# Transposed counts of a graph kernel: stored by the count stage, or fetched with transposing transfers

## The reference, cut to what matters

```python
def _hconv(x, W, b, src, dst, n):
    xt = x @ W
    ...
    m = jax.ops.segment_sum(xt[src], dst, num_segments=n) * Binv[:, None]
    out = jax.ops.segment_sum(m[dst], src, num_segments=n) * Dinv[:, None]
    return out + b
...
h = _prelu(_hconv(x, W1, b1, src, dst, n), a)
h = _hconv(h, W2, b2, src, dst, n) + x
```

## Time and profile before

| | us |
|---|---|
| median of 3 runs | 1770.72 |
| lowest, highest | 1768.19, 1774.01 |
| span of the profiled execution | 1767.3 |
| TensorE busy | 1590.3 |
| ScalarE busy | 1095.2 |
| VectorE busy | 1068.9 |
| DMA queue of SP, share of 16 engines | 32.7% |

### The profile page before, as it was taken

How to read it: one execution, slowest core, us unless ns; L and a number is a source line. 1 busy time by engine, 2 the same in 40 slices (tenths; PEclk the granted TensorE clock), 3 DMA queues, 4 the chain that set the end, 5 groups by cost and what they waited for, 6 DMA issues and landing times. The chain is left out here.

```text
span 1767.3 us, 35592 instructions
## 1 busy us (share of the span) xinstructions
PE 1590.3 (90%) x11957; PEld 1399.6 (79%) x11957; DVE 1068.9 (60%) x1881; ACT 1095.2 (62%) x2024; POOL 81.8 (5%) x116
## 2 busy tenths in 40 slices
PE   5777677599999999998999799999999999999697
PEld 4666666599999999996666599997779999777465
DVE  5598898679999999997455411122322112677662
ACT  1377778688888888885333466656665555567221
POOL 3000000000000000002000100000000000111213
PEclk9888898799999999998999999999999999999899
DMA  7315555345121221303000144445554444557212
GB/s 203 95 62 169 160 160 154 96 129 141 25 68 46 58 62 38 75 1 76 13 1 0 41 111 122 123 108 140 129 136 125 124 122 108 146 155 175 70 28 55
DMA packets 137572, 170.06 MB, mean 96 GB/s; under 512 B 20374, under 2 KB 129099, under 8 KB 137448
## 3 DMA queue, kind: packets, MB, share of 16 engines
q1 hardware_dynamic: 127538, 155.61, 32.7%
q0 software_dynamic: 6368, 9.36, 2.1%
q10 hardware_dynamic: 3542, 3.46, 0.8%
HBM read 114.58 MB, written 53.76 MB: 95 GB/s over the span
## 5 line engine op out<-in xcount | busy, mean ns | idle before, releaser
L1611 PE MATMUL ps_sets<-arena,kinds_mem 125*125 125x195 bf16 (+1 forms) x2500 | 447.2, 247 | 24.6 <-DVE kinds_mem L1370 16.7
L1354 ACT ACTIVATE kinds_mem<-ed_rows,es_mask 125x625 bf16<-125x625 f32 x500 | 367.0, 810 | 59.2 <-PE ps_sets L1617 31.0
L1617 PE MATMUL ps_sets<-arena,kinds_mem 125*125 125x195 bf16 (+1 forms) x2300 | 396.9, 248 | 0.0
L1611 PEld LDWEIGHTS ps_sets<-arena,kinds_mem 125*125 125x125 bf16 x2500 | 342.5, 137 | 31.6 <-DVE kinds_mem L1370 23.6
L2800 ACT ACTIVATE onewide<-ring 125x625 fp32r (+1 forms) x325 | 222.5, 720 | 168.7 <-PE oneps L2517 95.0
L1617 PEld LDWEIGHTS ps_sets<-arena,kinds_mem 125*125 125x125 bf16 x2300 | 308.2, 134 | 0.0
L2489 PE MATMUL oneps<-onewide,parts_a 125*128 125x376 f32 (+1 forms) x2000 | 293.1, 308 | 8.3 <-DVEq L2580 8.3
L2489 PEld LDWEIGHTS oneps<-onewide,parts_a 125*128 125x128 f32 x2000 | 291.2, 190 | 9.2 <-DVEq L2578 8.7
L2517 PE MATMUL oneps<-oneparts_b,onewide 125*125 125x512 f32 x1000 | 234.6, 395 | 0.0
L2517 PEld LDWEIGHTS oneps<-oneparts_b,onewide 125*125 125x125 f32 x1000 | 184.5, 185 | 48.6 <-DVE onefull L2652 1.9
L1362 DVE TENSOR_TENSOR kinds_mem<-kinds_mem,blk 125x2500 bf16<-125x2500 bf16 x120 | 182.4, 1520 | 33.9 <-ACT kinds_mem L1354 28.8
(11 more groups left out here) (451 smaller groups left out, 1903.8 us busy)
## 6 DMA issues: line engine op xcount, KB each, us to landing
ring<-counts SPq DMA_DIRECT2D x50, 683.6 KB
ring<-countsT SPq DMA_DIRECT2D x40, 683.6 KB
countsT<-kinds_mem SPq DMA_DIRECT2D x25, 683.6 KB
blk<-counts SPq DMA_DIRECT2D x20, 546.9 KB
counts<-blk SPq DMA_DIRECT2D x3, 3418.0 KB
counts<-kinds_mem SPq DMA_DIRECT2D x2, 3418.0 KB
ed_rows<-ed_dram SPq DMA_DIRECT2D x16, 273.4 KB
ring<-countsT SPq DMA_DIRECT2D x10, 410.2 KB
```

What stands on the lines that cost most here:

```text
L1354: return k.nc.scalar.activation(kinds_of(k)[:, slot, 0, :], k.ed_b[:, h, :], ACT.Relu, scale=MASK_SCALE, bias=k.es_mask[:, t, h:h + 1])
L1611: t_.matmul(out[0], kind[0], z[0], start=(t == 0), stop=False)
L1617: last = t_.matmul(out[1], kind[1], z[1], start=False, stop=(t == T - 1))
```

## The change

The count stage no longer makes or stores transposed counts: L839, L774, L877 and their semaphores are gone, with ScalarE's wait for `tr_stored`. SP's block store now waits for ScalarE's last copy of the block (`blk_done`) directly. `counts` becomes 16 rows longer (`PAD_ROWS`); GpSimd clears a buffer of zeros and SP stores it into these rows at the start of the stage.

Passes two and four read `counts` itself. Each chunk is fetched by five transposing transfers, one for each tile: the source is 640 rows (`RP`, fifteen more than the block needs) of 128 elements, with a row step of 3125 elements, the destination 128 partitions of 640 elements. In the last two blocks of pass four the source has 384 rows (`CUT`) or 256. The ring grows to 128 partitions and 640 elements a tile; some small vectors of the passes move into a buffer that is free by then. Passes one and three fetch as before.

```diff
@@ count_phase, ScalarE
-                    if not first:
-                        act.wait_ge(tr_stored, 32 * i)
                     for u in range(U):
                         hist_out(j, w, u)
                         if u == 0 and not first:
                             second_part(i - 1)
                         if u == 1:
                             first_part(i)
-                        if not first:
-                            tr_out(i - 1, TR_AFTER[u])
...
@@ count_phase, SP
+                sp.wait_ge(pad_set, 1)
+                for plane in (k.counts_wide, k.counts_low_wide):
+                    sp.dma_start(plane[N:N + PAD_ROWS, :], pad).then_inc(k.pad_stored, 16)
                 for j in range(U):
-                    with sp.Fori(0, U) as w:
-                        i = j * U + w
...
-                        for lo_, hi_ in SPLIT:
-                            sp.dma_start(k.countsT.rearrange("(t p) s -> t p s", p=P)[bass.ds(i, 1), lo_:hi_, :].rearrange("a p s -> (a p) s"),
-                                         tr[lo_:hi_, bass.ds(i % 2, 1), :].rearrange("p a s -> p (a s)")).then_inc(tr_stored, 16)
+                    sp.wait_ge(blk_done, U * U * (j + 1) + U)
                     if j < U - 1:
...
@@ convolutions_phase, SP
+                def transposed_in(s, slot, row, n_rows, at):
+                    plane = wide_counts[s // U]
+                    for w in range(U):
+                        t = (s % U) * U + w
+                        first = plane[row, t * P:(t + 1) * P]
+                        sp.dma_start_transpose(ring[:, slot, w, at:at + n_rows],
+                                               bass.AP(first.tensor, first.offset, [[N, n_rows], [1, 128]])).then_inc(c_in[s % U], 16)
...
                     sp.wait_ge(wide_done, U * (NS * (U * n + i) + s) + U)
-                    for lo_, hi_ in CSPLIT:
-                        sp.dma_start(ring[lo_:hi_, slot, :, :].rearrange("p a t d -> p (a t) d"), src[lo_:hi_]).then_inc(c_in[s % U], 16)
+                    if n % 2:
+                        transposed_in(s, slot, bass.ds(i * QB, RP), RP, 0)
+                    else:
...
@@ convolutions_phase, SP, last_counts_in
                     sp.wait_ge(wide_done, U * chunk + U)
-                    for lo_, hi_ in CSPLIT:
-                        sp.dma_start(ring[lo_:hi_, chunk % RB, :, c0:c1], src[lo_:hi_]).then_inc(c_in[s % U], 16)
+                    transposed_in(s, slice(chunk % RB, chunk % RB + 1), slice(i * QB + c0, i * QB + c0 + n_rows), n_rows, at)
```

More of the change, by code:

```diff
@@ L55 @@
 CSPLIT = ((0, 112), (112, P))
+RP = 640
+CUT = 384
+PAD_ROWS = RP - QB + 1
 class Env:
@@ L674, in _ @@
             def _(pool):
+                nc.gpsimd.memset(pad, 0.0)
+                nc.gpsimd.drain().then_inc(pad_set, 1)
                 clear_past(k, pool)
@@ L832, in histogram @@
                     last.then_inc(hist_done, 1)
[L834 to L845, removed]
+                for u in range(U):
+                    histogram(0, u)
+                with pe.Fori(1, T) as i:
                     for u in range(U):
                         histogram(i, u)
[L848 to L859, removed]
             @block.sync
@@ L1487, in masks @@
                         return
-                    if first and h == 0 and m == NM - 1:
-                        act.wait_ge(k.tr_stored, 32 * T + 64)
-                        act.sem_inc(act_passed, 1)
                     if m == 0 and part[0] == 0 and not first:
@@ L2316, in choice_ids, with convolutions_phase @@
     last.then_inc(s.ids_psum, 1)
-def convolutions_phase(k, name, counts, countsT, later):
+def convolutions_phase(k, name, counts, wide_counts, later):
     nc = k.nc
@@ L2338, in chunk_of, with loaded @@
         return Q_LAST - 1 + (i - U + 2) * len(LAST) + part
+    def loaded(n, chunk, s):
+        before = U * len(counts) * (32 * ((n + 1) // 2) + 16 * U * (n // 2))
+        return before + (16 * U if n % 2 else 32) * (len(counts) * (chunk - U * n) + s // U + 1)
     def sums_before(i):
@@ L2359, in convolutions_phase @@
         tab_i = sb(name + "tab_i", [P, T + NQ], I32)
-        num = sb(name + "num", [P, T], FP32)
-        one = sb(name + "one", [P, T], FP32)
-        inv = sb(name + "inv", [P, 2, T], FP32)
-        degree = sb(name + "degree", [P, T], FP32)
+        free = k.dst_exp[:, :, :, :].rearrange("p t h e -> p (t h e)")
+        num, one, degree = (free[:, c * T:(c + 1) * T] for c in range(3))
+        inv = free[:, 3 * T:5 * T].rearrange("p (j t) -> p j t", j=2)
         row_sums = sb(name + "row_sums", [P, U, NS, U], FP32)
@@ L3250, in program @@
             clear_past_phase(k)
-            convolutions_phase(k, "two", [k.counts, k.counts_low], [k.countsT, k.countsT_low], None)
+            convolutions_phase(k, "two", [k.counts, k.counts_low], [k.counts_wide, k.counts_low_wide], None)
         with nc.Else():
             enter_branch(nc)
-            convolutions_phase(k, "one", [k.counts], [k.countsT], k)
+            convolutions_phase(k, "one", [k.counts], [k.counts_wide], k)
         nc.end_all_ifs()
```

77 lines of the change are left out of this document (32 added, 45 removed).

## The result

| | before | after |
|---|---|---|
| median of the runs, us | 1772.37 (1768.19 to 1774.76, 4 runs) | 1850.24 (1849.04 to 1851.5, 4 runs) |
| ratio | | 1.0438, 95% interval 1.0422 to 1.0453 |
| span of the profiled execution, us | 1767.3 | 1847.3 |

The kernel became slower by 78 us, where I had forecast 36 (1807, with a range of 1773 to 1895). The direction and the range held, the size did not: it is more than double. The question for the experiments is therefore not whether the transposing transfers cost more than the count stage gives, but what makes them cost 95 us where I gave them 50.

The account below looks back on a forecast made before the run. VectorE was taken to bound the count stage, TensorE the convolution passes. Profiled 1767.3 - 14 (count stage) + 50 (pass four) = 1803.3, plus 3.4 to the runs' median: 1807 us, range 1773 to 1895.

Parts of the forecast that it names:

- Count stage, -14: Count stage: VectorE's four stops behind ScalarE's transposed-store waits go (-13.0 us), and its end moves earlier; -14 us, between -11 and -17.
- rival 3: Count stage gives nothing because ScalarE's stops fall to the wait for block stores instead; 1821 us, chance 0.02.
- T: Time in SP's queue from the start of one transposing transfer to the next in passes two and four; taken as 1.2 us.
- my formula: Passes two and four lose the larger of 175T - 160 and 100T - 73.4, plus 125T - 155 where T exceeds 1.24.
- the line: Packet time from two earlier rows: 10 ns plus 0.05 ns a byte, so 640 rows of 256 bytes take 0.92 us.
- The 0.4 us a chunk for address arithmetic: SP's loops in passes two and four: five times a 75 ns instruction, added to each chunk's five transfers.
- Pass two, 0: Pass two: the fetch takes 150.0 us against 154.2 now, so it is hidden, with 4 us to spare.
- Pass four, +50: Pass four: SP feeds chunks slower than TensorE needs them, 202.7 us against 152.7, a loss of 50 us.
- the signs: Pass four's later profile: ScalarE waits some 50 us for the ring, nearly all in the last 20 chunks, spaced 6 us.
- Rival 1: Passes two and four: transposing transfers flow as plain ones do, T under 0.83; 1757 us, faster, chance 0.11.
- Rival 2: Passes two and four: each transfer waits for the one before to land, T 1.5 to 2.2; 1892 to 2102 us, chance 0.08.
- Rival 4: Passes two and four: T between 0.83 and 0.94, gain and loss cancel; 1765 to 1776 us, chance 0.05.

## Why the prediction was right in sign and wrong in size

**Count stage, -14: right.** Measured 15.7 in the stage, and 13.4 as the median of an experiment of its own. The four stops behind the transposed stores are gone, tiles are VectorE from end to end, the last stop is 2.81 us, and rival 3 (nothing gained) is out. That a block store waits for the one before it (31.5 us in SP's list, in three waits) held nobody.

**T, 1.2 us: the step that failed.** It is the term of the sum that was mis-sized. I built T as issue plus data of a 640-row piece in turn, beside the middle of two far bounds. Issue turned out at 1.16 us by itself, 3.5 times the plain issue that I had taken as the floor, and the data runs beside it: 640 rows hold SP 38 ns longer than 128. Starts in pass two lay 1.37 us apart where I had 1.28 (1.2 and a fifth of the 0.4 us for a chunk's address arithmetic). In pass four they lay 1.40 apart in the mean where I had 1.23, and 1.34 without GpSimd's stores. In the terms of my formula, which has the arithmetic in its constants, T was 1.29 in pass two, and in pass four 1.36, or 1.30 without the stores.

A tenth more in T is a large step here, because everything above TensorE's need is lost in full. My own formula, 175T - 160 and 125T - 155, gives 79 + 6 us at these T, against 50 + 0 at what I assumed. The sum is then 1767.3 - 14 + 85 + 3.4 = 1842 us. The 8 us still missing are the slips in the constants that follow (10), less what the count stage gave beyond 14 us. So the formula was right in kind, and the middle of bounds as far apart as 0.33 and 2.2 was no ground for a sum as steep as this one.

One reading under T was off as well. The packets of the earlier trace rows had 1194 bytes in the mean (4.58 MB in 3837), not 1250. It mattered little: the line gave 23 ns for a row of 256 bytes and the changed kernel shows 20.8 (29504 packets in 64.0% of 16 engines' 60 us), so 640 rows are 0.83 us of data and not 0.92.

**The 0.4 us a chunk for address arithmetic** was the wrong picture too. The arithmetic fills about 0.2 us between two holds, 1 us a chunk, but taken out of the list it gave back 0.05 us a transfer, a quarter of itself, since SP's hold grew as the arithmetic went.

**Pass two, 0: wrong, +13.1.** There are two slips beside T. I took the length of my window, 154.2 us, for the length of the pass; it runs from 1173.92 to 1324.41 in the trace of before, so it is 150.5 us long, and the 4 us to spare were 0.5. And the first fill started 15.9 us ahead of the pass (1143.16 against 1159.08), not 18.5; 3 x 6.3 - 0.7 is 18.2 besides. With the measured terms, -15.9 + 171.1 + 1.8 of landing + 6.7 for the last chunk, the same working gives 163.7; it is 163.6. Rows of before:

```profile
1173.92 6.04 PE L2517 MATMUL oneps<-oneparts_b,onewide 125*125 125x512 f32 x25
...
1183.92 140.65 PE L2517 MATMUL oneps<-oneparts_b,onewide 125*125 125x512 f32 x600
1324.41 10.88 PE L2489 MATMUL oneps<-onewide,parts_a 125*128 125x376 f32 x74
```

**Pass four, +50: right in mechanism, +82.1.** SP's 175 transfers take 244.5 us instead of 216. Of these 28.5, some 18 are spacing (it is there without GpSimd's stores) and 10 are the stores. The working left these out altogether: I had them at no price, while the earlier trace rows already showed GpSimd busy 9.05 and 7.54 us in just these stretches. The rest is the shorter lead (2.5) and a later end (1.4). The later end has a term that I did not think of, TensorE's clock: its last ten matmuls took 4.9 us at a granted clock of 0.50, and 2.7 before at 1.00. Of the signs, the steps held (6.4 us whatever the size, 6 forecast), and SP waited for ScalarE nowhere in these two passes. ScalarE waited 85.7 us for the ring in the last 20 chunks; they have 65.8 of the 82.1 us, four fifths and not nearly all, for the loop part lost 16.3 already.

**The rivals.** Rival 1 (transfers flow as plain ones do) falls with the hold of 1.16 us, and with it, for this use, the sentence of the Trainium skill ("Advanced Engine Details and Errata", X-Bar Transpose (TRN2)) that transposing DMAs are as fast as regular ones: per instruction a factor 3.5 lies between them here, while in one large transfer the data flows quickly enough to be hidden (3.14 us for 640x640 in a period of 5.9). The 1309 ns for 128x128 of the Trainium skill ("VectorE: DVE Perf Modes", The three transpose paths) came nearer than my T: 128x128 held SP 1.12 us and starts lay 1.33 apart; its 1835 us were 15 short, mine 43. Rival 2 (each waits for its landing) had T from 1.5 up, and the spacing of 1.37 stays below it. The last transfer of pass two starts at 1313.0, and ScalarE, waiting for it, goes on at 1316.02: it lands 3.0 us after its start, while the starts before it follow each other in less than half of that. Rival 4 (T from 0.83 to 0.94) is out.

## What to carry to other kernels

Count the transposing transfers, not only their bytes: here each took SP at least 1.1 us, so make few and large ones, if need be by laying the data out in memory so that one transfer covers what five did. Before pricing a stream by a mean T, look how steep the sum is in T: where an engine is fed one chunk at a time and has no slack, every tenth of a microsecond counts a hundred times. When two versions are compared by a few microseconds, look first whether they start the changed stage at the same time: here 4 us lay ahead of it. And a pass is as long as the trace says from its first to its last matmul, not as long as the window in which it was looked at.

## What the runs showed of the hardware that I had not expected

- A transposing transfer held SP 1.12 us for 128x128 elements, 1.16 for 640x128 and 3.14 for 640x640 (medians in pass two); in the last 20 chunks of the run with one per chunk, where no store of GpSimd's was under way, 1.30 to 1.34 us for 256 rows by 640 columns and 1.53 to 1.60 for 384.
- Issued back to back with fixed addresses, transfers of 640x128 start only 0.05 us closer than with loop arithmetic between them: the hold grew from 1.16 to 1.27.
- While x_dram and out_dram rows leave on GpSimd's queue, single holds are longer: up to 3.2 us for a 640x128 transfer (2.4 at most in pass four without these stores), up to 6.7 us for one of 640x640.
- A copy from memory to memory in pieces of 256 bytes ran at 91 GB/s. It held SP 0.9 us itself; the next one behind it was held until about its end. Six copies held SP 227.5 us, the two ahead of the mixture stage 46.8.
- TensorE's granted clock was 0.50 (the lower of its levels, 1.2 GHz) over the count stage of the changed kernel, with 162 of 237 us busy (0.87 before, with 171), and 0.79 in the mean in the last 20 chunks, with 81 of 125 us busy. It cost nothing in the count stage, where VectorE waited for no other engine, and 2.2 us at the end of pass four, on the last ten matmuls, which no transfer hides.
